# Last stage: engine programs reordered, and three fp32r passes for the five products of the transposed rows

## What is computed

```python
x = x + _L0_gnn_ref(_layernorm(x), adj, ...)
x = x + _L0_ffn_ref(_layernorm(x), ...)
x = x + _L1_gnn_ref(_layernorm(x), adj, ...)   # relu(A_norm @ (H W^T + b))
x = x + _L1_ffn_ref(_layernorm(x), ...)
```

```python
h = relu(einsum('baf,efh->ebah', x, eW1) + eb1)     # 4 experts
h = relu(einsum('ebah,ehg->ebag', h, eW2) + eb2)
o = einsum('ebag,ego->ebao', h, eW3) + eb3
shared = relu(relu(x @ sW1 + sb1) @ sW2 + sb2) @ sW3 + sb3
gates = softmax(x @ gW + gb); topv, topi = top_k(gates, 2); topw = softmax(topv)
```

## Time and profile before

| | us |
|---|---|
| median of three runs | 1537.96 |
| lowest and highest of them | 1537.5, 1540.89 |
| profiled execution, its own time | 1536.0 |
| span of the profiled execution | 1534.2 |
| busy in the span: TensorE | 1303.0 |
| VectorE | 1153.8 |
| ScalarE | 916.0 |
| GpSimd | 797.0 |

### The profile page before, as it was taken

One profiled execution on the slowest core, in us unless ns is written; L12 is line 12 of the kernel. 1 busy time (PEld: TensorE's weight loads), 2 busy tenths in 40 slices (PEclk: granted clock), 3 DMA queues, 4 the chain that ended last, 5 costly groups with the idle time before them and its releaser, 6 DMA issues. The chain is left out here.

```text
span 1534.2 us, 26804 instructions
## 1 busy us (share of the span) xinstructions
PE 1303.0 (85%) x6416; PEld 910.6 (59%) x6416; DVE 1153.8 (75%) x3916; ACT 916.0 (60%) x1747; POOL 797.0 (52%) x750
## 2 busy tenths in 40 slices
PE   5888499962556999999999999159999999999998
PEld 4666266651444777777777777136565565655665
DVE  5787465559985999999999998347767777677763
ACT  1333244430005999999999998146667666676674
POOL 3543111123006777777777774566666666666620
PEclk9999655555777999999999999669999999999999
DMA  4554444440002223323222237212122221222210
GB/s 161 185 186 149 117 122 130 125 161 0 1 1 85 80 75 80 79 74 79 80 77 75 80 78 64 62 49 69 57 76 58 68 68 56 76 59 68 69 35 22
DMA packets 136461, 124.07 MB, mean 81 GB/s; under 512 B 14164, under 2 KB 115949, under 8 KB 135278
## 3 DMA queue, kind: packets, MB, share of 16 engines
q1 hardware_dynamic: 119021, 88.03, 18.9%
q0 software_dynamic: 17408, 35.69, 10.0%
HBM read 83.89 MB, written 39.77 MB: 81 GB/s over the span
## 5 line engine op out<-in xcount | busy, mean ns | idle before, releaser
L946 POOL DMA_INDIRECT exg<-xln_scratch,eidx x288 | 324.9, 1128 | 127.4 <-issue 69.1
L1249 POOL DMA_INDIRECT yg<-expert_rows_scratch,idx x256 | 247.2, 966 | 101.4 <-issue 77.8
L1100 DVE TENSOR_TENSOR ehl<-ehr,ehh 128x512 fp32r<-128x512 f32 x288 | 197.6, 686 | 28.5 <-ACT ehh L971 28.2
L968 ACT ACTIVATE ehr<-p_eh,bc 128x512 f32<-128x512 f32 x288 | 198.4, 689 | 26.3 <-PE p_eh L1010 18.6
L971 ACT ACTIVATE ehh<-ehr 128x512 fp32r<-128x512 f32 x288 | 182.1, 632 | 9.2
L1487 DVE SCALAR_TENSOR_TENSOR xtok<-yg,prob,xtok 128x128 f32 (+1 forms) x256 | 80.1, 348 | 124.5 <-DMA yg<-expert_rows_scratch,idx 116.6
L1256 POOL TENSOR_TENSOR root_l<-pre_l,mhalf 128x4 f32<-128x4 f32 x64 | 80.7, 1262 | 130.4 <-DVE pre_l L1507 130.4
L1008 PE MATMUL p_ey<-ehh,wh 128*128 128x512 f32 x288 | 126.8, 440 | 0.8 <-DVE ehl L1100 0.8
L1008 PE MATMUL p_eh<-exh,wh 128*128 128x512 f32 x288 | 125.7, 437 | 1.5 <-DVE exl L1095 1.5
L1348 PE MATMUL p_lh<-x4t,w 128*128 128x512 f32 x256 | 122.2, 601 | 0.0
L962 ACT ACTIVATE exh<-p_ex 128x512 fp32r<-128x512 f32 x72 | 41.9, 582 | 123.5 <-PE p_ex L1004 121.6
(11 more groups left out here) (207 smaller groups left out, 3089.8 us busy)
## 6 DMA issues: line engine op xcount, KB each, us to landing
expert_rows_scratch<-eyo SPq DMA_DIRECT2D x72, 256.0 KB
xtok<-in_x_tok SPq DMA_DIRECT2D x8, 1024.0 KB, 7.1
an<-in_a_t SPq DMA_DIRECT2D x16, 512.0 KB, 4.6
xln_scratch<-xl SPq DMA_DIRECT2D x16, 512.0 KB, 3.6
at<-in_a_t SPq DMA_DIRECT2D x32, 256.0 KB, 2.8
out<-outx SPq DMA_DIRECT2D x32, 256.0 KB, 2.5
wj<-in_w_grp SPq DMA_DIRECT2D x16, 321.0 KB, 4.2
exg<-xln_scratch,eidx POOLq DMA_INDIRECT x288
```

The lines of the kernel that those rows point to most:

```text
L946: pool.indirect_dma_start(out=xg[p][:, k, :], out_offset=None, in_=xln_d, in_offset=bass.IndirectOffsetOnAxis(ap=idx[p][:, k:k + 1], axis=0))\
L968: nc.scalar.activation(hr[c % 2][:, :], p_h[c][:, :], ACT.Relu, bias=bc[p][:, c:c + 1])\
L1100: nc.vector.tensor_tensor(hl[:, c, :], hr[c % 2][:, :], hh[:, c, :].bitcast(F32), ALU.subtract)\
L1249: pool.indirect_dma_start(out=yg[p][:, c, k, :], out_offset=None, in_=y_d, in_offset=bass.IndirectOffsetOnAxis(ap=idx[p][:, c, k:k + 1], a ...
```

## The change

It keeps what is computed, but makes the five products of x4t in another way, and moves steps of the engines' programs.

New data: x4h is x4t rounded to fp32r (ScalarE), x4l the rest (VectorE); w1h and w1l are the same for the five weights of those products, made once at the start of the stage. A product is then three passes, w1h by x4h, w1l by x4h, w1h by x4l.

```diff
+                    def up(c, e):
-                        product(c, e, [(p_h[e % 2][:, :], w1[:, e, :], x4t[:, :])])
+                        dst = p_h[e % 2][:, :]
+                        pe.wait_ge(h_ready, 8 * c + e + 1)
+                        nc.tensor.matmul(dst, w1h[:, e, :], x4h[:, :], start=True, stop=False)
+                        nc.tensor.matmul(dst, w1l[:, e, :], x4h[:, :], start=False, stop=False)
+                        if e == 0:
+                            pe.wait_ge(x4l_ready, c + 1)
+                        nc.tensor.matmul(dst, w1h[:, e, :], x4l[:, :], start=False, stop=True).then_inc(h_done, 1)
```

```diff
                         if complete:
                             roots(j + 1, 0)
+                        if more:
+                            rows(j + 1, q, 1, range(R // 2))
                         if aggregate:
                             roots(j - 1, 1)
                         if more:
-                            rows(j + 1, q, 1)
+                            rows(j + 1, q, 1, range(R // 2, R))
```

```diff
+                        if finish:
+                            act.wait_ge(rc_ready, 2 * j - 7)
+                            relu(j - 4, 5, rp[0][:, :], be[:, E1:E1 + 1])
                         if hidden:
                             act.wait_ge(t4_done, j - 2)
                             nc.scalar.activation(x4t[:, :], flat(p_tb), ACT.Copy).then_inc(x4t_ready, 1)
+                            act.wait_ge(x4t_ready, j - 2)
+                            nc.scalar.activation(x4h[:, :], x4t[:, :], ACT.Copy).then_inc(x4h_ready, 1)
                         if aggregate:
                             act.wait_ge(ag_done, j - 1)
                             nc.scalar.activation(agt[:, :], flat(p_ta), ACT.Copy).then_inc(agt_ready, 1)
+                        if finish:
+                            relu(j - 4, 6, rp[1][:, :], be[:, E1 + 1:E1 + 2])
+                            relu(j - 4, 7, hs[1][:, :], bs[:, 1:2])
...
                             relu(c, 4, hs[0][:, :], bs[:, 0:1])
-                            if finish:
-                                act.wait_ge(rc_ready, 2 * j - 6)
-                            relu(c, 5, rp[0][:, :], be[:, E1:E1 + 1])
-                            relu(c, 6, rp[1][:, :], be[:, E1 + 1:E1 + 2])
-                            relu(c, 7, hs[1][:, :], bs[:, 1:2])
```

```diff
+                        if finish:
+                            second(c - 1, 6, 1)
+                            product(c - 1, 7, [(p_h[1][:, :], ws[:, P:2 * P], hs[0][:, :])])
...
+                        if hidden:
+                            pe.wait_ge(x4h_ready, j - 2)
+                            up(c, 0)
                         if finish:
                             pe.wait_ge(cw_ready, j - 3)
                             nc.tensor.transpose(p_ta[:, 0, :], ...).then_inc(ct_done, 1)
                         if hidden:
-                            up(c, 0)
                             up(c, 1)
                         if finish:
-                            pe.wait_ge(cwt_ready, j - 3)
-                            spread(0)
-                            spread(1)
+                            spread(j, 0)
+                        if hidden:
+                            up(c, 2)
+                        if finish:
+                            spread(j, 1)
...
                         if hidden:
-                            up(c, 2)
                             up(c, 3)
...
-                            product(c, 4, [(p_h[0][:, :], ws[:, 0:P], x4t[:, :])])
+                            up(c, E1)
                             second(c, 5, 0)
-                            second(c, 6, 1)
-                            product(c, 7, [(p_h[1][:, :], ws[:, P:2 * P], hs[0][:, :])])
```

```diff
                         if hidden:
+                            dve.wait_ge(x4h_ready, j - 2)
+                            nc.vector.tensor_tensor(x4l[:, :], x4t[:, :], x4h[:, :].bitcast(F32), ALU.subtract)\
+                              .then_inc(x4l_ready, 1)
+                        if complete:
+                            dve.wait_ge(x2_ready, 2 * j + 2)
+                            dve.sem_inc(passed, 1)
+                            for r in range(R):
+                                stats(j, 0, r)
```

More of the change, by code:

```diff
@@ L1165, in build @@
             x4t = alloc(ctx, "x4t", [P, W])
+            x4h = alloc(ctx, "x4h", [P, W], F32R)
+            x4l = alloc(ctx, "x4l", [P, W], F32R)
+            w1h = alloc(ctx, "w1h", [P, E1 + 1, P], F32R)
+            w1l = alloc(ctx, "w1l", [P, E1 + 1, P], F32R)
             gr = alloc(ctx, "gr", [P, R, D])
@@ L1206, in build @@
             x4t_ready = sem("l_x4t_ready")
+            x4h_ready = sem("l_x4h_ready")
+            x4l_ready = sem("l_x4l_ready")
+            w1_s = sem("l_w1_s")
             hl_done = sem("l_hl_done")
@@ L1246, in _, with rows @@
                 def _(pool):
-                    def rows(j, p, c):
-                        for k in range(R):
+                    def rows(j, p, c, ks):
+                        for k in ks:
                             pool.indirect_dma_start(
@@ L1267, in body @@
                             pool.sem_inc(passed, 1)
-                            rows(j + 1, q, 0)
+                            rows(j + 1, q, 0, range(R))
                         if complete:
                             roots(j + 1, 0)
+                        if more:
+                            rows(j + 1, q, 1, range(R // 2))
                         if aggregate:
@@ L1273, in body @@
                         if more:
-                            rows(j + 1, q, 1)
+                            rows(j + 1, q, 1, range(R // 2, R))
                     pool.wait_ge(idx_ready, 1)
-                    rows(0, 0, 0)
-                    rows(0, 0, 1)
+                    rows(0, 0, 0, range(R))
+                    rows(0, 0, 1, range(R))
                     turns5(pool, NB, body)
@@ L1314, in body @@
                             last.then_inc(gr_ready, 1)
+                        if hidden:
+                            relu(c, 0, he[0][:, :], be[:, 0:1])
                         if finish:
@@ L1319, in body @@
                         if hidden:
-                            relu(c, 0, he[0][:, :], be[:, 0:1])
+                            relu(c, 1, he[1][:, :], be[:, 1:2])
                             act.wait_ge(d_ready, 2 * j - 5)
                             nc.scalar.activation(sm[1][:, :, :], sm[1][:, :, :], ACT.Exp).then_inc(exp_done, 1)
-                            relu(c, 1, he[1][:, :], be[:, 1:2])
                         if norm:
@@ L1357, in second, with spread @@
                                        (p_h[u % 2][64:128, :], w2[:, a + 1, :], he[a + 1][:, :])])
-                    def spread(pair_):
+                    def spread(j, pair_):
+                        if pair_ == 0:
+                            pe.wait_ge(cwt_ready, j - 3)
                         for k in range(R):
@@ L1437, in _ @@
                     dve.sem_inc(out_ready, 1)
+                    dve.sem_inc(rc_ready, 1)
                     for p in range(2):
@@ L1459, in _ @@
                     nc.vector.scalar_tensor_tensor(wg1[:, :], wg1[:, :], 1.0 / D, wgcn[:, :], ALU.mult, ALU.add)\
+                      .then_inc(set_, 1)
+                    nc.vector.tensor_copy(w1h[:, 0:E1, :], w1[:, :, :])
+                    nc.vector.tensor_copy(w1h[:, E1, :], ws[:, 0:P]).then_inc(w1_s, 1)
+                    dve.wait_ge(w1_s, 1)
+                    nc.vector.tensor_tensor(w1l[:, 0:E1, :], w1[:, :, :], w1h[:, 0:E1, :].bitcast(F32), ALU.subtract)
+                    nc.vector.tensor_tensor(w1l[:, E1, :], ws[:, 0:P], w1h[:, E1, :].bitcast(F32), ALU.subtract)\
                       .then_inc(set_, 1)
@@ L1559, in body @@
                         if complete:
-                            stats(j, 0, 1)
+                            variance(j, 0)
                         if hidden:
@@ L1564, in body @@
                               .then_inc(d_ready, 1)
-                        if complete:
-                            stats(j, 0, 2)
-                            stats(j, 0, 3)
-                            averages(j, 0)
-                            variance(j, 0)
                         if aggregate:
@@ L1574, in body @@
                             nc.vector.tensor_tensor(batch, batch, gr[:, :, :], ALU.add).then_inc(x3_ready, 1)
+                        if aggregate:
+                            dve.wait_ge(x3_ready, j - 1)
+                            dve.sem_inc(passed, 1)
+                            for r in range(R):
+                                stats(b, 1, r)
                         if hidden:
@@ L1585, in body @@
                         if aggregate:
-                            stats(b, 1, 1)
+                            variance(b, 1)
                         if hidden:
```

26 lines of the change are left out of this document (7 added, 19 removed).

## The result

The changed kernel has a median of **1521.81 us** over four runs (1520.2 to 1525.62). Beside it, on the same chip, the kernel before had 1539.37 over four runs (1537.5 to 1540.89). The ratio is 0.9899, with a 95% interval of 0.9884 to 0.9914. The profiled span fell from 1534.2 to 1519.7 us, by 14.5.

What follows compares the result with a forecast made beforehand. Bound: the ring of gathers, VectorE's choices and statistics, and roots, 15.93 us a turn. 28 x (0.40 - 0.92) = -14.6, tail -1.9 and start +0.3 make -16.2 us, giving 1521.8 against median 1537.96; range 1505 to 1535.

Steps and rivals of the forecast that it cites:

- the ring: Last stage's loop of gathers, their landing, VectorE's choices and statistics, roots, gathers again: 15.93 us per turn, taken as the bound.
- The split's gain: GpSimd, end of root 0 to last gather's start: 6.18 us falls to 5.26, gaining 0.92 us per turn.
- Root 0 stays at 1.55: GpSimd's first root of a turn waits for VectorE's addition of gr and still takes 1.55 us.
- rival 1: On GpSimd, root 0 slips ahead of VectorE's addition, 0.55 us shorter; ring 14.86 us, total 1506 us; chance 0.2.
- VectorE loses 0.40 us: VectorE ahead of root 0 gets x4l and rearranged statistics: 0.40 us lost per turn, bounds 0.34 and 0.60.
- rival 3: TensorE becomes the bound, 15.3 or 15.9 us a turn; sign: no wait for gathers left; chance 0.1.
- The passes save 1.05 us per turn of TensorE: On TensorE, three fp32r passes take 0.69 us against 0.90 per fp32 product; five products save 1.05 us.
- TensorE's floor is 14.7: TensorE's turn: 13.8 us of work plus 0.9 of waits, 14.7 us, still under the ring.
- spread's wait: TensorE's spread waits for the combine weights, copied after ScalarE's first relu: 0.9 us or less per turn.
- x4l's wait: TensorE's third pass of the first product waits 0.6 us for VectorE's x4l, overlapping spread's wait.
- Once, and the tail: Making w1's high and low halves at stage start costs +0.3 us; the four tail turns without gathers give -1.9 us.
- Rival 2: On GpSimd, a root behind gathers sits out a 0.99 us pause, costing 2.29; total 1549.6 us; chance 0.12.

Runs made afterwards that it cites:

- g6: Changed kernel with fp32 products instead of the passes, and ScalarE's copy of cwt ahead of relu 0: 1613.01 us, 0.9499 of the kernel before.
- cwt first: Changed kernel with ScalarE's copy of the combine weights (cwt) ahead of relu 0: 0.9488, 0.9484 and 0.9511 of the kernel before.

## Why the prediction was right, and where it was not

The predicted 1521.8 us is the measured 1521.81. **The number is right because two errors of 11 us cancel:** the turns became shorter by 25.2 us where I had 14.6, and seven falls of the clock, which I had not at all, took 11.2 back. What is left is luck as well: between the profiled executions the span fell by 14.5 where I had 16.2, and the after kernel's median lies 0.3 us above its profiled execution where I had added 2.0. Step by step:

- *The bound before was the ring, and the split is the change's lever.* Shown, on the slower chips: the split alone gives 4.6 to 4.7 of 5.2%, and without it the time is 0.7% above before. That the split would carry most of it on the first chip too is argued from the traces and was not run there.
- *The split's gain, 0.92 us, with a root behind gathers at 1.30.* The root took 1.04, the lower bound. The stretch from root 0's end to the last gather is 5.44 us (1303.76 to 1309.20), forecast 5.26, as the gather behind root 0 took 1.40 where I had 1.02. With root 0 itself 0.51 shorter, root 0's start to the last gather's start fell from 7.73 to 6.48 us: a gain of 1.25. My bound for the root rested on the claim that no root began sooner than 0.99 us behind a gather; the trace of the kernel before has one 0.47 us behind (1185.37).
- *Root 0 stays at 1.55.* Wrong. It has the length that rival 1 gave it, but not by rival 1's race: the addition of gr, which it collided with, now waits 1.03 us for ScalarE's gr and starts at 1303.78, after the root.
- *VectorE loses 0.40 us.* From at's start to the variance it is 2.63 us (1299.84 to 1302.47) where it was 2.28: a loss of 0.35.
- *The ring.* In the turn shown it is 15.93 - 1.25 + 0.35 = 15.03 us by these rows, not 15.4 (an estimate). But this turn has a gather stretched to 1.40 us by the addition of gr, and when that addition comes is set by TensorE, which makes what gr is taken from. In five other turns the gather isn't stretched and the first choice follows the last gather at once (2.87 to 2.95 us), and there the ring shows its own length: 14.64 to 14.75 us from first choice to first choice. One of them, 14.67:

```profile
1282.37 0.35 DVE L1520 SCALAR_TENSOR_TENSOR xtok<-yg,prob,xtok 128x128 f32 x1 [0.55 <-issue]
...
1297.04 0.35 DVE L1520 SCALAR_TENSOR_TENSOR xtok<-yg,prob,xtok 128x128 f32 x1 [0.17 <-issue]
```

  So the ring fell by some 1.2 us, from 15.9 to 14.7. On the average choices come every 15.1 in ordinary turns, and VectorE's wait for gathers is not 1.3 us but nearly nil. That is rival 3's sign.
- *The passes save 1.05 us per turn of TensorE.* Mis-sized. I took the spacing of two fp32r passes, 0.23, three times. The first pass of each product takes 0.31 to 0.34 to the next, the third 0.32 where a spread or a second layer follows it, and a product takes 0.78 to 0.89, on the average 0.83, against 0.90. By that alone five would save 0.35; the turns without gathers give 0.79 in the new order, where a fp32 product takes 0.94 and its neighbours 0.08 longer each, and 0.54 in the old.
- *TensorE's floor is 14.7.* **This is the term that failed.** It is 14.85 + 0.38 for the order - 0.79 for the passes + 0.57 for the wait = 15.01 in the tail, and 15.1 with the wait of 0.62 in the turns with gathers, which is the turn. The 0.38 I had put at nothing: the order was to "cost nothing while TensorE has slack". The two spreads apart take 1.17 us in g6 where together they took 1.03, and the five fp32 products 4.68 where they took 4.49. I bounded spread's wait by 0.9 and let x4l's wait of 0.6 overlap it. The wait for x4l isn't there: the third pass starts at 1302.49, and x4l was written at 1301.13. The wait for cwt is, 0.62 us.
- So **TensorE became the bound**, as in rival 3, but at 15.1 and not at 15.3 to 15.9. Only one of its two waits came, while the order cost more and the passes saved less. I gave rival 3 0.1 because those waits "share their time"; what decided was that the ring fell by more than I thought. That TensorE bound is read from its tail turn of 15.01 and from its only wait; no run on the first chip took it away.
- *Once, and the tail.* Forecast +0.3 and -1.9; the records give +1.1 and -1.7, or +0.3 and -0.9 without the transpose's change of place. The first two turns of the tail are 15.0, not 14.5: the wait for cwt is 0.53 us in the rows there too. My -1.9 doesn't follow from its own terms either: 4 x 0.35 and 0.8 make 2.2.
- *What no case of mine had* is the granted clock. I took 2.4 GHz for the whole stage, and misread: the 26th and 27th slice (959 to 1036 us), the stage's start, stand at 6 there, and a 9, for 90% or more of 38 us, can hide a fall of 3.4 us. Seven falls cost 11.2 us. Without them the kernel would be near 1511, in my range but with the gain per turn of a case that I gave 0.2.
- *Rival 2*, a pause on GpSimd between gather and root, is refuted: the root begins 0.03 us behind the gather, in the first turns as well.

Open: why the clock falls in seven turns and not in the others; what the stops on the other chips are, and why the split is worth more beside them (the trace shows TensorE's readers released late, not the reason, and that only while gathers run); and what cwt first and the split alone bring to the time on a chip without stops. By the ring's 14.7 against the turn of 15.1, cwt first could bring 0.4 us per ordinary turn there, some 11 us, beside what it does to the clock; by the floors 14.85 and 15.09 the split alone could be some 6 us faster than the whole change. Both are estimates.

## What to carry to other kernels

When a ring and a busy engine lie within 1 us of each other per turn, work out both floors with every new wait in them before asking which part of a change pays: here the ring fell from 15.9 to 14.7 and the next engine stopped it at 15.1. Price a short pass by the spacing it has in the sequence where it will stand, not by the spacing in a run of its like, and count what a new order costs the engine itself. Read each version's floor where the other bound is absent, here in the turns without gathers, on whatever chip. Fill the wait in front of a late instruction with work that others wait for; splitting one group of gathers in two was nearly the whole gain on the chips where it ran alone. The costly part of the change, the passes, could be left out there without a loss that the times can tell; where TensorE alone binds they are worth 0.5 to 0.8 us of a turn.

## What was unexpected of the hardware

- TensorE's granted clock fell to 1.2 GHz for some 3.4 us in seven turns, with the engine busy for 96% of a window of the stage (335.87 of 350 us). The last four falls are 92.2 us apart, six turns each, and all are at about one place of the turn. The kernel before, also busy for 96%, had none.
- A root directly behind gathers costs nothing extra: 0.03 us from the gather's end, 1.04 us long. The next gather comes 0.20 us behind it and is the one that stretches: 1.40 us where it begins 0.18 us behind an addition on VectorE, 1.02 where it doesn't (1307.88). In 17 turns the gather behind root 0 begins 0.15 to 0.35 us after the addition of gr, and each time it ends 0.89 or 0.90 us after the addition does, as root 0 did in the kernel before (1304.47 and 1305.36 in the turn shown). The Trainium skill, SBUF — State Buffer, section "SBUF: two separate sides", has VectorE with two SBUF inputs and GpSimd exclude each other for a whole instruction, whichever starts first. These 17 turns agree. In four others both begin within 0.01 us of each other; there the gather takes 1.02 us and the addition 0.71 to 0.73 instead of 0.69, so it did not wait for the gather's end (1274.32 against 1274.62).
- The kernel before ran 10 to 11% slower in the three groups, all of it in one stage and there only in the turns with gathers, with readers of TensorE's results released up to 5.8 us late (ScalarE's hs in the kernel without the split).
